# A graph layer in steps of 512 edges: TensorE's transposes and segment sums moved to later steps, ScalarE's work reordered

## The reference

```python
p1 = jnp.tanh(p @ pp_W1 + pp_b1) @ pp_W2 + pp_b2
inter = jnp.concatenate([p1[idx_i], p1[idx_j]], axis=-1)
inter = inter @ pi_W1 + pi_b1
inter = inter @ pi_W2 + pi_b2
inter = inter @ pi_W3
inter = inter.reshape(inter.shape[0], D, N_BASIS)
i1 = jnp.einsum('ecb,eb->ec', inter, basis)
i1 = jnp.tanh(i1 @ ii_W1 + ii_b1) @ ii_W2 + ii_b2
out = jax.ops.segment_sum(i1, idx_j, num_segments=p1.shape[0])
```

## Time and profile before

| | |
|---|---|
| median of 3 runs | 1993.1 us (1991.51 to 1993.95) |
| span of the profiled execution | 2703.6 us; the page gives no other time for it |
| TensorE busy in it | 1947.7 us, 72% |
| VectorE, ScalarE, GpSimd busy | 1439.4, 1089.0, 1483.3 us |
| mean granted clock of TensorE | 0.852 of 2.4 GHz |

### The profile page before, as it was taken

One profiled execution on the slowest core, in us unless ns is written; L12 is line 12 of the kernel. 1 busy time (PEld: TensorE's weight loads), 2 busy tenths in 40 slices (PEclk: granted clock), 3 DMA queues, 4 the chain that ended last, 5 costly groups with the idle time before them and its releaser, 6 DMA issues.

```text
span 2703.6 us, 54970 instructions
## 1 busy us (share of the span) xinstructions
PE 1947.7 (72%) x20012; PEld 1270.4 (47%) x20012; DVE 1439.4 (53%) x1939; ACT 1089.0 (40%) x2419; POOL 1483.3 (55%) x1581
## 2 busy tenths in 40 slices
PE   4112987777777777777777777777777777787788
PEld 3101654444544544544445444455444444554556
DVE  4302875555555555555555555555555554555556
ACT  2211653434443343444444444444443343444344
POOL 4773025555655555665656566666655555555551
PEclk9555998888988888898988888988988788788889
DMA  4311222222221221222222222222222222222221
GB/s 86 80 28 31 58 46 43 44 45 42 50 49 39 48 47 41 51 50 43 50 46 45 49 49 45 49 48 45 50 46 45 44 46 43 44 44 42 42 42 45
DMA packets 261709, 127.00 MB, mean 47 GB/s; under 512 B 183561, under 2 KB 233720, under 8 KB 261448
## 3 DMA queue, kind: packets, MB, share of 16 engines
q1 hardware_dynamic: 209967, 74.11, 13.1%
q0 software_dynamic: 50048, 51.35, 10.4%
q10 hardware_dynamic: 1558, 0.15, 0.1%
HBM read 119.47 MB, written 6.00 MB: 46 GB/s over the span
## 4 chain that ended last, share of the span: by engine, by line
PE 66%; issue 19%; another core or an unknown queue 8%; ACT 5%; DVE 1%; DVEq 0%; ACTq 0%
PE bank L1337 34%; PE bank L1320 10%; PE bank L1344 7%; PE bank L1427 6%; PE spread_ps L1329 5%; PE bank L1304 3%; ACT tt_sb L702 2%; ACT st_sb L714 2%; PE bank L1352 0%; DVE o_sb L945 0%; PE spread_ps L1166 0%; ACT t_sb L705 0%; DVE acc_all L899 0%; DVE loc_bc L893 0%
## 5 line engine op out<-in xcount | busy, mean ns | idle before, releaser
L526 POOL DMA_INDIRECT u_rows<-u_tab,src_e x1436 | 1357.4, 945 | 1102.8 <-PE bank L1320 750.9
L1337 PE MATMUL bank<-o_sb,g_sb 128*64 128x256 f32 x6256 | 943.3, 453 | 153.2 <-issue 144.5
L945 DVE TENSOR_TENSOR o_sb<-st_sb,spread_ps 128x2048 f32<-128x2048 f32 x391 | 889.7, 2275 | 229.3 <-remote 111.3
L714 ACT ACTIVATE st_sb<-bank,s_bias 64x256 f32<-64x256 f32 x1564 | 733.1, 469 | 182.2 <-PE bank L1320 90.6
L1009 DVE TENSOR_TENSOR hot_t<-loc_bc,bank 126x512 bf16<-126x512 bf16 x391 | 268.4, 687 | 942.6 <-remote 615.3
L1337 PEld LDWEIGHTS bank<-o_sb,g_sb 128*64 128x64 f32 x6256 | 522.3, 162 | 434.7 <-issue 307.9
L702 ACT ACTIVATE tt_sb<-bank,z_bias 128x256 f32<-128x256 f32 x391 | 185.0, 473 | 706.1 <-PE bank L1337 364.4
L1344 PE MATMUL bank<-ident,tt_sb 128*128 128x128 f32 x782 | 183.3, 319 | 369.8 <-issue 211.1
L705 ACT COPY t_sb<-bank 128x256 f32<-128x256 f32 x391 | 146.1, 374 | 569.3 <-PE bank L1344 306.8
L1427 PEld LDWEIGHTS bank<-hot,t_sb 128*65 128x65 f32 x3128 | 224.4, 143 | 184.5 <-issue 182.1
L1427 PE MATMUL bank<-hot,t_sb 128*65 128x42 f32 x3128 | 274.5, 239 | 19.4 <-issue 18.6
(11 more groups left out here) (148 smaller groups left out, 361.9 us busy)
## 6 DMA issues: line engine op xcount, KB each, us to landing
loc_bc<-loc_tab SPq DMA_DIRECT2D x391, 126.0 KB
u_rows<-u_tab,src_e POOLq DMA_INDIRECT x1436
v_win<-v_tab SPq DMA_DIRECT2D x391, 15.8 KB
basis<-edge_attr SPq DMA_DIRECT2D x24, 256.0 KB
v_tab<-acc_all SPq DMA_DIRECT2D x6, 336.0 KB
basis<-u_tab,src_e POOLq DMA_INDIRECT x100
u_tab<-basis SPq DMA_DIRECT2D x6, 224.0 KB
x_sb<-x SPq DMA_DIRECT2D x1, 1120.0 KB
```

What stands on the lines that cost most here:

```text
L526: pool.indirect_dma_start(out=u_rows[:, g % UR, j, :] if g >= AHEAD else first_u[:, g - XG, j, :], out_offset=None, in_=u_tab[:, :], in_of ...
L714: last = nc.scalar.activation(tiles[h * D:(h + 1) * D, j], s_ps[part].rearrange("p (q a e) -> p q a e", q=2, a=TILES), ACT.Identity, bias= ...
L945: return nc.vector.tensor_tensor(o_sb[:, r, :, :].rearrange("p c (j e) -> p j c e", j=TILES), st_sb[:, r, :].rearrange("p (j e) -> p j e", ...
L1337: last = nc.tensor.matmul(z_ps[h * D:(h + 1) * D, 0:2 * P], g_sb[:, c, :], o_sb[:, r, c, 2 * h * P:(2 * h + 2) * P], start=(c == 0), stop= ...
```

## The change

The transposes of t write to bank 5, which nothing else used in the loop, so z no longer waits for the copy of t. In TensorE's step the transposes are those of group n-3 and the sums those of group n-4, and the order within a step is s(n), sums(n-4), t(n-3), spread(n-1), z(n-2). ScalarE's step is now: copy of t(n-3), tanh(n-2), s(n). VectorE makes `hot` and adds the sums one step later. There is one step more.

```diff
-        z_ps, t_ps = bank[6][:, 0:2 * P], bank[6][:, 2 * P:2 * P + TILES * D]
+        z_ps, t_ps = bank[6][:, 0:2 * P], bank[5][:, 0:TILES * D]
...
-        STEPS = range(NG + 5)
+        STEPS = range(NG + 6)
...
-            def make_t(g):
+            def make_tanh(g):
                 act.wait_ge(z_ready, g + 1)
                 if g >= 2:
                     act.wait_ge(t_ps_ready, g - 1)
                 tanh_z(g % 2).then_inc(tt_ready, 1)
+
+            def make_t(g):
                 act.wait_ge(t_ps_ready, g + 1)
...
                 for n in STEPS:
-                    if has(n) and n < TURN:
-                        make_s(n)
+                    if has(n - 3):
+                        make_t(n - 3)
                     if has(n - 2):
-                        make_t(n - 2)
-                    if has(n) and n >= TURN:
+                        make_tanh(n - 2)
+                    if has(n):
                         make_s(n)
...
+                if of(4):
+                    pe.wait_ge(t_ready, seen(4))
...
+                    last.then_inc(seg_ready, 1)
+                if of(3):
+                    pe.wait_ge(tt_ready, seen(3))
+                    t_transposes((u - 3) % 2).then_inc(t_ps_ready, 1)
...
                 if of(2):
                     pe.wait_ge(o_ready, seen(2))
-                    if of(3):
-                        pe.wait_ge(t_ready, seen(3))
                     z_group(u % 2).then_inc(z_ready, 1)
```

More of the change, by code:

```diff
@@ L1035, in _ @@
                 for n in STEPS:
-                    if n == 4:
+                    if n == 5:
                         dve.wait_ge(acc_zero, 2)
-                    if has(n - 4):
-                        g = n - 4
+                    if has(n - 5):
+                        g = n - 5
                         start = dve.value_load(base_row[0:1, g:g + 1], min_val=EARLY if g >= LATE_G else 0,
@@ L1047, in _ @@
                         pick_t(n + 1)
-                    if has(n - 2):
-                        r = n - 2
+                    if has(n - 3):
+                        r = n - 3
                         if r >= HR:
@@ L1397, in step @@
                     newest()
+                if of(4):
+                    pe.wait_ge(t_ready, seen(4))
+                    if first and u == 4:
+                        pe.wait_ge(hot_ready, seen(4, 1))
+                    pe.wait_ge(hot_ready, seen(4))
+                    if of(5):
+                        pe.wait_ge(acc_done, seen(5))
+                    if last_pass:
+                        b, r = divmod(n + u - Y_STEP, 4)
+                        if r == 0 and 1 <= b <= BATCHES:
+                            pe.wait_ge(y_ready, b)
+                        if 0 <= b < BATCHES:
+                            y_early(b, r)
+                    for j in range(TILES):
+                        last = nc.tensor.matmul(seg_ps, t_sb[:, (u - 4) % 2, j, :], hot[:, (u - 4) % HR, j, :],
+                                                start=(j == 0), stop=(j == TILES - 1))
+                    last.then_inc(seg_ready, 1)
+                if of(3):
+                    pe.wait_ge(tt_ready, seen(3))
+                    t_transposes((u - 3) % 2).then_inc(t_ps_ready, 1)
                 if of(1):
```

## The result

The changed kernel takes 3350.45 us (median of 4 runs, 3346.1 to 3355.24) against 1993.53 us before: ratio 1.681, 95% interval 1.679 to 1.684. The forecast was 3660 us in a range of 3000 to 4130.

What follows compares the result with a forecast made beforehand. The prediction took TensorE's own work, 4.10 us a step, to bound the kernel before. For the changed kernel it summed 267 us around the steps and 390 x 8.7 us to 3660 us, range 3000 to 4130 us.

Steps and rivals of the forecast that it cites:

- What the change adds: On ScalarE, the copies of s(n) wait behind tanh(n-2), so TensorE pauses 2.44 us before s; 6.65 us a step against 4.10.
- not slower: ScalarE finishes the copies of s(n) before z(n-2) ends, so TensorE has no pause; 1864 us to no gain; 2%.
- The step at the upper clock: One chain through TensorE and ScalarE at the upper clock: 2.22 + 1.99 + 2.44 = 6.65 us, 2861 us in all.
- The clock: TensorE's pause behind every z lowers its granted clock to between 0.6 and 0.75, making a step 8.7 us.
- clock rivals: TensorE's clock mostly stays up, 2861 to 3350 us, 18%; or stays down in nearly every step, around 4105 us, 15%.
- mostly up: TensorE's clock mostly stays up: below 7.9 us a step, 2861 to 3350 us; chance 18%.
- down in every step: TensorE's clock stays down in nearly every step: over 9.4 us a step, around 4105 us; chance 15%.
- share of 0.64: Part taken of the difference between 6.65 us (upper clock) and 9.84 us (lower clock) a step, giving 8.7 us.
- second rival: TensorE's clock stays down in nearly every step, around 4105 us, 15%; the argument against: z alone occupies TensorE 3.4 us.
- The 267 us around the steps: Time outside the 390 steps: 256.4 us up to the first z and about 10 us behind the last.
- What bounds the kernel now: TensorE's own work, 4.10 us a step; a timed run's further 0.33 us unexplained, GpSimd's gathers one candidate.
- What it moves: TensorE runs the same matmuls in another order; VectorE's hot and addition go one step later and VectorE stays hidden.

Runs made afterwards that it cites:

- two tiles: The changed kernel with both engines' orders kept, s in banks 4 and 5 in turn, t_ps back in bank 6 with z's wait: 2032.22 us, ratio 1.021.
- filled run: The changed kernel with ten unused ident-by-ident matmuls put behind z in TensorE's pause: 2578.58 us.
- run with three gathers: The kernel before with three instead of four gathers per group from group 32 on, every fourth tile's source rows left out: 1709.25 us, ratio 0.858.

## Why the prediction was right, and where its numbers were off

*What the change adds* was right in every link. Forecast: 0.06 us between the last copy and s, no idle time ahead of the transposes, 950 us ahead of L1306. Measured: 0.15 us, 0.0, and 952.4 us. Only the first of these is off, and it is small. The runs with ScalarE's order put back, with two tiles, and with ScalarE's order alone each show that the late copies behind the single `s_ps` are the cause. The rival *not slower* fell: ScalarE ran in its program's order.

*The step at the upper clock* was 6.65 us in the sum and is 6.32 us in the filled run. I took sums, transposes and s from the old order; in the new one s's second part, the sums and t are 0.54, 0.45 and 0.35 us from start to start instead of 0.64, 0.64 and 0.37. At the lower clock it is the same: 9.84 us in the sum, 9.3 to 9.5 us in the 161 slowest steps.

*The clock* was the right direction and nearly the right size. Forecast 0.6 to 0.75 granted, measured 0.73 in the long stretch; forecast 8.7 us a step, measured 8.36. Both clock rivals fell: mostly up would have been under 7.9 us a step, down in every step over 9.4. The share of 0.64 between the two ends was a guess, and that it fits is partly luck: with the measured ends, 6.32 and about 9.4, 8.36 us is a share of 0.66. One argument against the second rival misread a row: z at the lower clock takes 3.6 us, not 3.4. The rule from the Trainium skill ("TensorE: Matmul & The Clock Gate", "HAM oscillation — how this bites in real kernels") that I set beside it (a pause in every tile brings the clock down in every tile) the trace bears out in part: there is a pause in every step, the clock is down 54% of the time, and only 40 steps are as short as the upper level makes them.

*The 267 us around the steps* were the largest single error. The first z comes at 80.9 us, not 256.4, and about 10 us lie behind the last one's start. I had seen that the profiled execution was 710 us too long and threw out its steps in the gathering stretch, but I kept its first part. That part was stretched as well: in the profile of the run with only the bank moved, whose first part is the same program, the first z comes at 79.9 us; the first part is 4% of the time, not an eighth as said ahead of the prediction. What held that one execution up so, first and last, stays open. The 310 us between 3660 and 3350 are 267 - 91 = 176 us here and 390 x (8.7 - 8.36) = 133 us in the steps.

*What bounds the kernel now* was wrong, and by the same mistake. With 267 us set aside I found 4.43 us a step for a timed run, 0.33 over TensorE's 4.10, and left its cause open with GpSimd's gathers as one candidate, which, I wrote, must be quicker in a timed run. With 91 us the step is 4.9 us, about the pace of four gathers of 1.25 us, which the first groups have behind them before they are needed; they are not quicker at all. The run with three gathers shows it (1709 us). This did no harm to the forecast, since a step of 8 us covers 5.0 us of gathers, but it also means that nothing the change removes could have made the kernel faster: not the bank (1993.14 us), and not the transposes' wait; together I had priced them at up to 129 us.

*What it moves* was wrong. I wrote that VectorE stays hidden, and that on TensorE the same matmuls only run in another order. Behind the pause VectorE does stay hidden; without it, the new order closes the ring of 4.75 us through VectorE's addition, and costs 262 us where the gathers don't cover it. And TensorE's own step became shorter, 3.84 instead of 4.10 us, which I had put at nothing. I had asked whether each moved operand is ready earlier, not for whom the moved instruction makes others wait.

## What to carry to other kernels

When an instruction is moved behind a wait on an in-order engine, everything after it inherits that wait; look for a buffer with a single copy among what it releases, since there the two engines' orders close into a chain. Count such rings edge by edge for every single-buffered tile that a reordering touches. And before timed runs are explained with a profile whose span is far from them, check each stretch of it, the first one too: a second execution of nearly the same kernel is worth more than any correction.

## What the runs showed of the hardware

- GpSimd starts a gather of 128 rows every 1.25 us (0.94 us busy and 0.30 us between two) in the run with only the bank moved, and four of them per step set the pace of the kernel before.
- Filling a pause of 2.47 us with 2.5 us of useless matmuls took the granted clock from 0.73 to 0.99 and the time from 3350 to 2579 us. As long as the wait itself can't be removed, that is a cheap remedy. The Trainium skill ("TensorE: Matmul & The Clock Gate", "HAM oscillation — how this bites in real kernels") advises, for a matmul with few rows, to restructure the loop so that TensorE's clock stays up, or to pad the rows. The run agrees in that added work kept the clock up.
- A GpSimd gather of 128 rows went from 950 to 1013 ns on average, single ones to 2.4 us, when two VectorE instructions of about 0.3 and 0.7 us read a constant from SBUF rather than from PSUM and the addition moved ahead of them. The long gathers are those that overlap the shorter of the two. The Trainium skill ("GPSIMD Engine Reference", "Specifications") says that GpSimd shares its SBUF interfaces with VectorE and that they contend where a VectorE instruction has two SBUF inputs; the longer gathers agree.
